# Two constant products ahead of every pair of the second gather and of every late static tile

## The reference, cut to what matters

```
N, D, NE = 6250, 256, 100000;  E, F, K = 16, 512, 2
xn  = layernorm(x)
h   = xn @ W.T
x1  = x + segment_sum(edge_weight[:, None] * h[dst], src)     # edges come sorted by dst
xn2 = layernorm(x1)
logits  = xn2 @ gate_w + gate_b;  top 2 of 16, softmax over the two
moe     = sum over the two experts of weight * (relu(xn2 @ w1[e] + b1[e]) @ w2[e] + b2[e])
y       = xn2 + moe
out     = x1 + layernorm(y) * gamma + beta
```

## Time and profile before

| Stretch of the span | us | what runs |
|---|---|---|
| 0 to 520 | 520 | layer norm, sort of the edges, static tiles 0 to 135 between the batches |
| 520 to 553 | 33 | static tiles 136 to 151, last lists stored |
| 553 to 573 | 20 | tables of the second gather loaded and transposed |
| 573 to 626 | 53 | static tiles 152 to 195 |
| 626 to 1814 | 1188 | second gather: 640 tiles, 49 windows |
| 1814 to 2404 | 590 | gating, experts, final sum |

### The profile page before, as it was taken

One profiled execution on the slowest core, in us unless ns is written; L12 is line 12 of the kernel. 1 busy time (PEld: TensorE's weight loads), 2 busy tenths in 40 slices (PEclk: granted clock), 3 DMA queues, 4 the chain that ended last, 5 costly groups with the idle time before them and its releaser, 6 DMA issues. The chain is left out here.

```text
span 2404.0 us, 33977 instructions
## 1 busy us (share of the span) xinstructions
PE 1508.3 (63%) x7875; PEld 1206.6 (50%) x7876; DVE 970.1 (40%) x2547; ACT 645.8 (27%) x1788; POOL 1204.3 (50%) x1170
## 2 busy tenths in 40 slices
PE   5256977564445565555565546464644799998975
PEld 3245866452334343333343434343433799897864
DVE  7995799472112222222222132121317333332338
ACT  5741266330000110101010100101015344443456
POOL 0045558786655555555555444545552355454434
PEclk9595589686668676877677767677876999999988
DMA  4112212224522222222222222222236222224346
GB/s 154 62 54 82 77 52 66 72 66 142 179 79 72 70 70 70 70 70 70 70 70 70 70 61 65 72 66 74 72 70 190 86 71 77 94 85 159 118 145 229
DMA packets 121466, 215.63 MB, mean 90 GB/s; under 512 B 21001, under 2 KB 82756, under 8 KB 121281
## 3 DMA queue, kind: packets, MB, share of 16 engines
q0 software_dynamic: 52864, 140.45, 19.9%
q1 hardware_dynamic: 53664, 56.14, 7.0%
q10 hardware_dynamic: 14880, 18.35, 2.3%
HBM read 172.32 MB, written 42.54 MB: 89 GB/s over the span
## 5 line engine op out<-in xcount | busy, mean ns | idle before, releaser
L470 POOL DMA_INDIRECT hbuf<-xn_rows,ix x640 | 614.9, 961 | 574.2 <-DVE ix L420 217.8
L549 PE MATMUL bank<-hbuf,picks 128*128 x1640 | 535.1, 477 | 549.8 <-SPq L458 274.4
L549 PEld LDWEIGHTS bank<-hbuf,picks 128*128 128x128 f32 x1640 | 363.6, 237 | 714.1 <-issue 660.4
L491 DVE TENSOR_SCALAR picks<-iota_two,marks 128x256 f32<-128x256 f32 x640 | 239.5, 420 | 920.6 <-remote 616.4
L737 POOL DMA_INDIRECT fbuf<-xn_rows,first_tables x196 | 230.1, 1174 | 130.0 <-PE bank L1261 66.9
L627 ACT ACTIVATE agg<-bank 128x256 f32<-128x256 f32 x49 | 18.8, 385 | 863.3 <-PE bank L549 565.5
L1845 PE MATMUL bank<-rowsT,w_sb 128*128 128x128 f32 x1744 | 216.3, 278 | 19.1 <-issue 19.1
L1845 PEld LDWEIGHTS bank<-rowsT,w_sb 128*128 128x128 f32 x1744 | 212.2, 193 | 31.0 <-issue 26.3
L1855 PE MATMUL bank<-w_sb,hT 128*128 128x256 f32 x872 | 209.2, 382 | 0.9 <-ACT hT L1803 0.6
L1781 POOL DMA_INDIRECT expert_out<-y_sb,to_i x112 | 111.4, 995 | 192.6 <-DVE y_sb L1890 188.0
L1279 PE MATMUL bank<-work 128*128 128x192 bf16 x1568 | 154.8, 254 | 75.2 <-DVE work L1067 57.1
(11 more groups left out here) (293 smaller groups left out, 1729.0 us busy)
## 6 DMA issues: line engine op xcount, KB each, us to landing
w_sb<-in_L_ffn_w_dram ACTq DMA_DIRECT2D x28, 512.0 KB
hbuf<-xn_rows,ix POOLq DMA_INDIRECT x640
first_sums<-x SPq DMA_DIRECT2D x49, 128.0 KB
first_sums_back<-first_sums SPq DMA_DIRECT2D x7, 896.0 KB
xn_rows<-xn SPq DMA_DIRECT2D x7, 896.0 KB, 4.6
x<-in_x_dram SPq DMA_DIRECT2D x6, 896.0 KB
ya<-expert_out SPq DMA_DIRECT2D x5, 896.0 KB, 5.3
yb<-expert_out SPq DMA_DIRECT2D x5, 896.0 KB, 7.2
```

The source lines that it names most:

```text
L470: pool.indirect_dma_start(hbuf[:, 1 + j, k, :], None, xn_dram, bass.IndirectOffsetOnAxis(ap=ix[:, 2 * j + k:2 * j + k + 1], axis=0)).then_ ...
L491: s = v.tensor_scalar(picks[:, j % 2, k, :], iota_two[:], marks[:, 0, 2 * j + k:2 * j + k + 1], marks[:, 1, 2 * j + k:2 * j + k + 1], ALU. ...
L549: m = nc.tensor.matmul(bk[q][:, 0:D], picks[:, j, k, q * P:(q + 1) * P], hbuf[:, ds(place + j, 1), k, :].rearrange("p s d -> p (s d)"), st ...
```

## The change

Each pair that is handled in the loop of a window (not the window's last quad) gets two further products ahead of its own, after the wait for `pair_in`: identity times a constant table of 256 columns, into bank 6, which nobody reads at that time. Each static tile after the batches gets the same two products into bank 7, ahead of its own waits. Bank 7 is no longer used for turning tables, so that five banks are left for it.

```
-        TURNED = 6
+        TURNED = 5
 
         def turned_1(b):
             return bk[2 + b % TURNED][:, 0:2 * P]
...
-            def quad(s, q):
+            def quad(s, q, kept_busy):
                 place = s & (PR - 1)
                 for j in range(2):
                     pe.wait_ge(pair_in, s + j)
+                    if kept_busy:
+                        for k in range(2):
+                            nc.tensor.matmul(bk[6][:, 0:2 * P], ident[:], iota_two[:], start=True, stop=True)
                     for k in range(2):
                         m = nc.tensor.matmul(bk[q][:, 0:D], picks[:, j, k, q * P:(q + 1) * P],
...
                 with pe.Fori(first, end, 2) as s:
-                    for m in quad(s, q):
+                    for m in quad(s, q, True):
                         m.then_inc(used, 1)
 
-                for m in quad(end, q):
+                for m in quad(end, q, False):
                     pass
...
-                def sum_to(tiles):
+                def sum_to(tiles, kept_busy=False):
                     nonlocal used
                     while used < min(tiles, FTILES):
                         w, t = divmod(used, FT)
                         if t == 0 and w >= 2:
                             pe.wait_ge(first_summed, w - 1)
+                        if kept_busy:
+                            for k in range(2):
+                                nc.tensor.matmul(bk[7][:, 0:2 * P], ident[:], iota_two[:], start=True, stop=True)
                         pe.wait_ge(first_picked, used + 1)
                         pe.wait_ge(xn_gathered[used % RH], 16 * (used // RH + 1))
...
-                sum_to(SORT_TILES + 16)
+                sum_to(SORT_TILES + 16, True)
...
-                sum_to(FTILES)
+                sum_to(FTILES, True)
                 gather_tensor(pe)
```

## The result

| | median us | runs | ratio to before, 95% interval |
|---|---|---|---|
| before | 2385.49 | 4 (2364.69 to 2874.64) | |
| the change | 2526.63 | 4 (2516.6 to 2538.71) | 1.0625 (1.053 to 1.0719) |
| the change again, on another chip (after_again below) | 2532.23, beside 2378.77 | 4 and 7 | 1.068 (1.0604 to 1.0757) |

One run of the kernel before, at 2874.64 us, was a slow one and is in no ratio. I had said 2601 us in a range of 2420 to 2800, slower with 0.86. Direction and place held, and so did the mechanism in the main; the size was too large: 218 us over before, against 141 and, the second time, 153.

A forecast was written before the change was run, and what follows sets the result against it. The prediction took POOL's pauses in the second gather, waiting on PE's late raises, as the bound. 2405.79 + 198 (pauses) + 20 (static tiles) = 2624 us profiled; the median lies 22.65 lower, 2601 us, range 2420 to 2800.

The forecast's parts named there:

- The bound: Second gather, 1188 us: no engine full; about 380 us are POOL pauses, 10 us each, which PE's work can lengthen or shorten.
- Term 1: Second gather's pauses: the one pair POOL's restart waits for grows by 1.67 us at clock 0.50.
- Term 2: Second gather: one more pair falls into each pause; with term 1 and windows' work 5.2 us, over 38 pauses +198 us.
- Static tiles and banks: Ahead of the second gather: tiles 136 to 151 cost 0, tiles 152 to 195 +20 us, five banks 0.
- The rule of the clock: Second gather: the skill's rule that activity releases the throttled clock, so more products would mean more time at 2.4 GHz.
- Rival 1: Second gather: clock stays up throughout, 2357 us, or standing covers everything, 2385 to 2425; no change to be told; chance 0.09.
- Rival 3: Second gather: all products on the path, PE's late raises later with each record ahead; 2823 us (2720 up); chance 0.12.
- Rival 4: Second gather: denser PE gets raises through at once, pauses go, stage 806 or 937 us, whichever longer; 2150 us; chance 0.05.

The follow-up runs named there:

- after_again: The changed kernel unaltered, run again beside the kernel before on another chip: 2532.23 us beside 2378.77, ratio 1.068.
- loop_only: The changed kernel with further products only in the second gather's loop, none at static tiles, six banks: 1980.79 us, ratio 1.0058 to the kernel before.
- static_only: The kernel before with further products only at the 60 static tiles, five banks, loop as before: 1990.78 us, ratio 1.0123.
- ahead: The changed kernel with the loop's further products moved ahead of the wait for the pair: 2010.1 and 2001.07 us, ratios 1.0155 and 1.0146 to before.
- small: The changed kernel with the loop's further products cut to 16 columns from 256, as many records: 1996.87 and 1985.64 us, ratios 1.0163 and 1.0074 to before.
- spaced_change: The changed kernel with a 128x256 memset on POOL ahead of each gather of the second gather: 2127.18 us beside 1962.0 for before, ratio 1.0823.
- spaced_16: The kernel before with a 128x16 memset on POOL ahead of each gather of the second gather: 1994.32 us, ratio 1.012.

## Why the prediction came out right, and where it was off

- **The bound.** "The pauses are what a change of PE's work can lengthen": held. POOL's idle grew by 130.6 and 152.1 us in the two pairs of profiles, the spans by 110.8 and 168.6, and where there are no pauses the loop's products cost nothing that can be told (loop_only, 1.0058).
- **Term 1, the pair of the pause: +1.67 us.** Held in the pause shown, 9.93 against 8.26 us; the agreement to the hundredth is luck.
- **Term 2, one more pair falls into the pause, together 5.2 us.** This is the term that was mis-sized. Over 38 pauses the stage grew by 112.6 / 38 = 3.0 us and 134.3 / 38 = 3.5 us, the pauses themselves by 3.1 and 3.7. I had counted a pause as one pair at the low clock, to which a second comes. I took that from the pause of 8.26 us and called the next one "the same again"; it is not: PE makes three pairs from 1046.96 on the earlier trace rows and two more before POOL's start, and DVE starts 1.6 us after POOL's last issue, not 3.2. By the table in the section on the result a mean pause held 3.6 to 3.9 real pairs before and 4.5 after. So 0.6 to 0.9 of a pair more fell into it, near the one that I took; but it was not paid at the low clock: with 3.8 to 3.9 pairs of constants in it the granted clock in the pauses rose from 0.61 to 0.77, and the pauses grew by 3.1 and 3.7 us, no more than about what these constants take at the high clock alone (3.9 x 0.95 = 3.7 us, an estimate from the earlier trace rows). That the sum came within the range is in part two errors against each other: too few pairs in a pause, and too low a clock for them.
- **Static tiles and banks: +20 us.** Right in size and place: 17 to 18 us in tiles 152 to 195 on both kinds of chip. For tiles 136 to 151 and the turning of the tables I had 0; there the profiles differ by more than the change could be seen in.
- **The rule of the clock.** Rival 1 asked for the clock to stay up. It went to 0.82, and to 0.98 with free raises. It gave something back: the real products became 58 us cheaper, and the pauses grew by less than the constants' price at the low clock. But it did not pay for the constants with held raises, and with free raises, where POOL sets the pace, it saved nothing: as the prediction put it, a pair with its constants at the high clock (1.9 us) takes no less than a bare one at the low clock (1.67). The Trainium skill's rule ("TensorE: Matmul & The Clock Gate", section on what is actually happening) that activity releases the throttle agrees with these rows; that the release is worth its activity is not in the rule, and not in the rows.
- **Rival 3**, raises that get later with each record ahead of them, did not come: the delays of DVE's starts sum to 549 us against 600, and to 552 against 586.
- **Rival 4**, raises that come through at once, is what chips 2 and 3 do without the change too. Where they do, the stage takes 823 us, near the 806 that I gave as POOL's floor. But the change does not bring it about: at 0.82 of the clock DVE's "remote" is 567.1 us, against 616.4.
- The forecast held for the kind of chip that the profile came from. It would have been wrong by some 600 us for the other kind (2601 against the 1980 to 2000 or so that loop_only, static_only and ahead point to), and no number in it says so; only the same kernel on another chip does.

**What stays open:** why PE's raises are held in some groups of runs, and whether it is the chip; whether the spacing of gathers or the memset itself frees them; whether it is the records or the time of the constants that lengthens a pause; and what the loop part alone, the place of the products, and the change with spaced gathers are worth with held raises: loop_only, ahead, small and spaced_change all ran with free ones.

## What to carry to other kernels

Work that is to keep TensorE's clock up does harm between the arrival of its data and the raise that others wait for: there it doubles PE's links in the chain that a pause consists of, and the higher clock gave back only part (that it would help in the time in which TensorE stands was not tested where it matters). One pause read closely does not stand for all: count them before a term is built on one. Before a wait is priced, ask whether the semaphore's rise is as late as the instruction that causes it ("remote"): if not, the cure lies with whoever holds up the rise, here POOL's run of gathers, and it can help to do that work more slowly. And take a profile of the same kernel from a second chip before a stage of 1188 us is believed: it can be one of 823.

## What the runs showed of the hardware that I had not expected

- The same kernel takes 1960 us on two chips and 2380 us on a third (and where the first profile was taken), and most of it is one stage, 1188 or 1159 us against 823 (by the profile of spaced_16, the nearest to before with free raises).
- On the slower kind PE's raises reach the others late, in the stretch shown 10 us and at most 18.6 and 19.7 us in the two profiles of before, while POOL issues gathers 1.26 us apart; in the pauses shown they are all there about 3.2 us after POOL's last issue ends. In the same stage single register steps of PE's sequencer take up to 1425 ns, against 60.
- With gathers 1.45 us apart on the same chip these steps are back at 60 ns at most, though raises are still up to some us late.
- The Trainium skill ("NOTIFIC — the notification-queue block", section "Overflow: three behaviours, one of which stalls the engine") says that a full ring of notification records can, in one of its modes, stall the engine that writes them; no run here shows whether that is what happens.
